# A gated cross-attention block with a mixture of experts on one core: PE sums the expert terms of three tiles, ACT copies the sums out, and the four engines get a new order of work

## What is computed

```python
x = x + tanh(g_xattn[0]) * xattn(layernorm(x), ctx, ctx, Wq, Wk, Wv, Wo)       # 16 heads of 64, causal
x = x + tanh(g_ffn[0]) * ffn(layernorm(x), ...)
# ffn, row by row:
h = rmsnorm(x, gamma1); q = h @ Wq + bq; k, v = split((h @ Wdown + bdown) @ Wup + bup)   # (rows, 16, 8) each
att = softmax(einsum('bthd,btgd->bthg', q, k) / sqrt(8)); out = einsum('bthg,btgd->bthd', att, v)
x = x + (out @ Wo + bo)
h2 = rmsnorm(x, gamma2); gate = softmax(h2 @ Wg + bg)
return x + einsum('btd,edf,bte->btf', h2, We, gate)                            # We is 8 x 128 x 128
```

## Time and profile before

| what | us |
|---|---|
| median of 3 runs | 265.44 |
| lowest and highest | 265.3 and 267.71 |
| the profiled execution's own time | 265.66 |
| its span, first to last instruction | 263.8 |

### The profile page before, as it was taken

The page is one execution under the profiler, slowest core; times in us unless marked ns, Lnnn a source line. Parts: engine busy times, 40 slices in busy tenths (PEclk is TensorE's granted clock), DMA queues, the critical chain, the costliest instruction groups (busy, mean ns, idle before and its releaser), DMA issues.

```text
span 263.8 us, 7717 instructions
## 1 busy us (share of the span) xinstructions
PE 236.0 (89%) x3154; PEld 167.0 (63%) x3154; DVE 195.0 (74%) x335; ACT 168.3 (64%) x498; POOL 159.0 (60%) x169
## 2 busy tenths in 40 slices
PE   5989989898999999998999999989999988851781
PEld 3765778586768585857676776867685665530360
DVE  0236644198989796979798832989897999999925
ACT  2437634756686868785877778667868767651452
POOL 4104041619196877878587376691968778739644
PEclk9999999999999999999999999999999999995698
DMA  6990000000000000000000000000000000000000
GB/s 212 369 307 6 2 4 0 6 0 2 0 5 10 2 14 0 4 10 5 11 2 12 2 10 4 10 5 0 2 12 2 11 4 14 0 0 0 12 10 20
DMA packets 6016, 7.28 MB, mean 28 GB/s; under 512 B 477, under 2 KB 4830, under 8 KB 5982
## 3 DMA queue, kind: packets, MB, share of 16 engines
q1 hardware_dynamic: 5550, 6.16, 7.2%
q10 hardware_dynamic: 432, 0.64, 0.7%
HBM read 5.88 MB, written 0.92 MB: 26 GB/s over the span
## 4 chain that ended last, share of the span: by engine, by line
PE 77%; ACT 9%; DVE 7%; issue 3%; DMA 1%; POOL 0%; SPq 0%; DVEq 0%; ACTq 0%; POOLq 0%
PE ps_a L825 47%; PE ps_c L825 11%; PE ps_b L825 9%; PE ps_e L825 5%; PE ps_b L877 3%; ACT exb L462 2%; DVE ps_e L616 2%; DMA cT<-in_ctx_t 1%; ACT probs L407 1%; ACT probsT L414 1%; ACT v_sb L396 1%; DVE psums L583 1%; PE ps_c L921 1%; DVE exb L684 1%; ACT aT L401 1%
## 5 line engine op out<-in xcount | busy, mean ns | idle before, releaser
L268 POOL TENSOR_TENSOR probs<-probs,prinv 120x672 f32<-120x672 f32 x16 | 24.3, 1517 | 48.3 <-DVE prinv L587 48.2
L277 POOL TENSOR_TENSOR prod<-fqkv 128x1280 f32<-128x1280 f32 (+1 forms) x14 | 38.5, 2752 | 1.9 <-DVE fqkv L601 0.7
L825 PE MATMUL ps_a<-aT,wo_sb 128*128 128x112 f32 x256 | 32.9, 281 | 2.1 <-ACT aT L401 1.3
L825 PEld LDWEIGHTS ps_a<-aT,wo_sb 128*128 128x128 f32 x256 | 29.9, 191 | 4.2 <-ACT aT L401 2.0
L644 DVE TENSOR_REDUCE ps_e<-prod 128x128 f32<-128x2048 f32 x14 | 31.9, 2281 | 0.4 <-POOL prod L288 0.4
L616 DVE TENSOR_REDUCE ps_e<-prod 128x256 f32<-128x2048 f32 x14 | 32.0, 2284 | 0.0
L825 PE MATMUL ps_a<-wv_sb,cT 128*64 128x512 f32 x128 | 31.4, 606 | 0.0
L825 PE MATMUL ps_a<-cT,wk_sb 128*128 128x224 f32 x128 | 28.9, 379 | 1.3 <-DMA cT<-in_ctx_t 1.3
L401 ACT COPY aT<-ps_a 128x448 f32<-128x448 f32 x32 | 15.5, 536 | 20.4 <-PE ps_a L825 20.4
L825 PEld LDWEIGHTS ps_a<-cT,wk_sb 128*128 128x128 f32 x128 | 24.6, 203 | 5.6 <-DMA cT<-in_ctx_t 2.9
L825 PE MATMUL ps_a<-xT,wqc 128*128 128x224 f32 x128 | 27.0, 359 | 0.6 <-ACT qT L390 0.6
(11 more groups left out here) (136 smaller groups left out, 468.9 us busy)
## 6 DMA issues: line engine op xcount, KB each, us to landing
xp_sb<-in_xp SPq DMA_DIRECT2D x1, 896.0 KB, 7.8
out<-out_sb SPq DMA_DIRECT2D x14, 64.0 KB, 1.5
xT<-in_x_t SPq DMA_DIRECT2D x1, 784.0 KB, 9.1
cT<-in_ctx_t SPq DMA_DIRECT2D x1, 784.0 KB, 10.6
wv_sb<-in_wv SPq DMA_DIRECT2D x1, 512.0 KB, 7.7
wo_sb<-in_wo SPq DMA_DIRECT2D x1, 512.0 KB, 12.1
fwe_sb<-in_fwe SPq DMA_DIRECT2D x1, 512.0 KB, 8.8
fw_sb<-in_fw SPq DMA_DIRECT2D x1, 266.0 KB, 12.4
```

The lines of the kernel that those rows point to most:

```text
L268: nc.gpsimd.tensor_tensor(pr[0:TG, NC:C, :, 0:S], pr[0:TG, NC:C, :, 0:S], prinv[p % 2][0:TG, NC:C, :].unsqueeze(3).to_broadcast([TG, C - N ...
L277: nc.gpsimd.tensor_tensor(prod1[:, 0:hp, :, :], t[:, D:2 * D].rearrange("p (g d) -> p g d", g=FH).unsqueeze(1).to_broadcast([128, hp, FH, ...
L825: return nc.tensor.matmul(o, lhsT, rhs, start=start, stop=stop, skip_group_check=True)
```

## The change

1. PE takes over `outputs` for tiles 10, 11 and 12 (`PE_OUT`): `output_sums(f)` runs ten matmuls, the identity against each of the ten terms of `exb`, which add up in one PSUM region (`ps_a` for tile 10, `ps_e` for the others), and ACT copies the sum to `out_sb` (`late_out`). POOL's twelve instructions for the three tiles are gone. Tile 11's sums stand on PE between `turn_x2` and `gate_logits` of tile 13, and tile 12's at the very end.
2. The ten identity matmuls of `stay_warm` are gone.
3. The last tile's gate exponentials are written to PSUM, so `last_gating` reads them there.
4. The slots are put in another order. Steps 2 to 13: PE runs `first` behind `turn_probs` and both expert halves behind `attend`, the upper one first, `shift` ahead of `bias_o`; ACT makes `x1_copy` behind `turned_probs`, and `kv_copy` between the two halves of `experts`; DVE runs `gate_logits` behind `weighted` and `head_sums` ahead of `gate_sum` and `scaled_qkv`; POOL runs `weighted` ahead of `first_scale`. Steps 14 and 15 and the end likewise, as the rows below and the diff show.

The diff, cut to its core (the products' new helper functions hold the same operands as before):

```diff
+PE_OUT = (10, 11, 12)
-STAY_WARM = 10
...
+        def gate_exp(f):
+            return ps_c[:, 1, 256 + E:256 + 2 * E] if f == NT - 1 else gexp[f % 2][:, :]
+
+        def out_sum(f):
+            return ps_a[:, 1, 0:D] if f == PE_OUT[0] else ps_e[:, 0, 0:D]
...
+                elif f in PE_OUT:
+                    sp.wait_ge(s["late_out"], f - PE_OUT[0] + 1)
...
             products(prior)
             first_scale(last)
+            products(last)
             weighted(prior)
-            products(last)
             second_scale(third)
-            outputs(third - 1)
             gating(third)
             weighted(last)
             second_scale(prior)
-            outputs(third)
+            last_residual(last)
             gating(prior)
             second_scale(last)
-            last_residual(last)
-            outputs(prior)
...
+            def late_out(f):
+                act.wait_ge(s["out_summed"], f - PE_OUT[0] + 1)
+                act.wait_ge(stored[f % 2], 16 * (f // 2))
+                nc.scalar.copy(out_sb[f % 2][:, :], out_sum(f)).then_inc(s["late_out"], 1)
...
+            x1_copy(last)
             o_copy(third)
-            x1_copy(last)
+            x2_copy(third)
+            kv_copy(last)
             head_exps(prior)
-            x2_copy(third)
+            late_out(PE_OUT[0])
             squares(third)
-            kv_copy(last)
+            head_exps(last)
             gate_exps(third)
             o_copy(prior)
-            head_exps(last)
+            experts(third, 1)
+            x2_copy(prior)
             squares(prior)
-            experts(third, 1)
+            o_copy(last)
             experts(third, 0)
-            x2_copy(prior)
+            squares(last)
             gate_exps(prior)
-            o_copy(last)
+            x2_copy(last)
             experts(prior, 1)
-            x2_copy(last)
-            squares(last)
             experts(prior, 0)
             gate_exps(last)
+            late_out(third)
             experts(last, 0)
+            late_out(prior)
...
-                nc.vector.tensor_scalar(gate[f % 2][:, :], gexp[f % 2][:, :], ginv[f % 2][:, :], r2[f % 2][:, :],
+                nc.vector.tensor_scalar(gate[f % 2][:, :], gate_exp(f), ginv[f % 2][:, :], r2[f % 2][:, :],
...
+            def output_sums(f):
+                pe.wait_ge(s["lo_ready"], f + 1)
+                pe.wait_ge(s["hi_ready"], f + 1)
...
+                for e in range(E + 2):
+                    ins = mm(out_sum(f), ident[:, :], exb[f % XB][:, e, :], start=(e == 0), stop=(e == E + 1))
+                ins.then_inc(s["out_summed"], 1)
...
             new_y(NP - 1)
+            first(last)
+            bias_o(third)
             turn_o(third)
-            bias_o(third)
             new_o(third)
-            first(last)
             turn_x2(third)
+            output_sums(PE_OUT[0])
             gate_logits(third)
+            bias_o(prior)
+            expert_half(third, 0)
             turn_o(prior)
+            new_o(prior)
             expert_half(third, 1)
-            bias_o(prior)
-            new_o(prior)
-            expert_half(third, 0)
             turn_x2(prior)
+            gate_logits(prior)
             expert_half(prior, 0)
-            gate_logits(prior)
-            stay_warm(prior)
+            turn_o(last)
             bias_o(last)
-            turn_o(last)
+            new_o(last)
             expert_half(prior, 1)
-            new_o(last)
             turn_x2(last)
+            output_sums(third)
             gate_logits(last)
             expert_half(last, 1)
             expert_half(last, 0)
+            output_sums(prior)
```

More of the change, by code:

```diff
@@ L512, in _ @@
                 if t < NP:
-                    attended(t, 0)
                     attended(t, 1)
+                if fc is not None:
+                    experts(fc, 0)
                 if fa is not None:
@@ L517, in _ @@
                 if fc is not None:
-                    experts(fc, 0)
                     experts(fc, 1)
@@ L789, in _ @@
             last, prior, third = NT - 1, NT - 2, NT - 3
+            new_x1(NP - 1)
             products(prior)
-            new_x1(NP - 1)
             logits(prior)
             new_x2(third)
+            scaled_qkv(last)
             shifted_logits(prior)
-            scaled_qkv(last)
+            products(last)
             weighted(prior)
-            products(last)
-            head_sums(prior)
+            logits(last)
             head_scales(prior)
             gate_logits(third)
+            shifted_logits(last)
+            head_sums(prior)
+            gate_sum(third)
             normed_heads(prior)
-            logits(last)
-            gate_sum(third)
-            shifted_logits(last)
-            new_x2(prior)
             weighted(last)
             head_scales(last)
+            new_x2(prior)
             head_sums(last)
+            normed_heads(last)
             gate_logits(prior)
-            normed_heads(last)
+            new_x2(last)
             gate_sum(prior)
-            new_x2(last)
             gate_logits(last)
@@ L1019, in _ @@
                     turn_o(fc)
-                    bias_o(fc)
                 if t < NP:
@@ L1023, in _ @@
                 if fc is not None:
+                    bias_o(fc)
                     new_o(fc)
```

109 lines of the change are left out of this document (56 added, 53 removed).

## The result

The changed kernel takes 269.19 us (median of 4, 268.2 to 269.66), the kernel before beside it 266.48 (4, 265.3 to 267.71): a ratio of 1.011 with a 95% interval of 1.0068 to 1.0151, slower by 1.1%. (The prediction started from 265.44, the median of three executions; beside the changed kernel it took 1.0 us more.) The profiled execution took 268.92 us with a span of 266.8, against 265.66 and 263.8 before.

A forecast was written before the change was run, and what follows sets the result against it. PE's list was taken to bound the body, DVE the next stretch, a chain through all engines the end. Body -0.9 and end +0.2 gave -0.7 from 265.66, so 265.0, or 264.8 us against the median; range 262.6 to 267.4.

The forecast's parts named there:

- Full steps: Eight body steps with both a first and a third stage: PE's new order costs +0.05 us each, +0.4 us together.
- Step 9: Body step without `first`: `attend` waits uncovered, 3.96 us becomes 4.77, so +0.8 us.
- Steps 2, 3 and 11: Body steps without expert halves: `first` fills the 0.69 us in which PE idled, -2.1 us for the three.
- What hides the rest: Body: waits for POOL, DVE and ACT stay covered, by 0.4 us at `turn_probs` and 0.2 to 0.5 us elsewhere.
- Rival (c): Body margin used up, likely `turn_probs` waiting for POOL or `bias_o` for ACT; eight steps pay, 268.5 us; chance 0.08.
- Rival (f): Body: more gain than reckoned, PE's short stops vanish with the new addresses; below 262.8 us; chance 0.12.
- DVE's stretch: Steps 14 and 15 up to tile 13's heads: DVE's list loses small gate instructions and short waits, -0.6 us, heads at 250.8.
- The last chain: Tile 13's heads to last sum: clock returns at 251 to 254, x2 at 254.0; +0.2 us for the end.
- Rival (b): End: PE's clock comes back later than 254 us, end +1.4 us, launch 265.9 us; chance 0.14.
- a few tenths: Very end: tile 12's sum, copy and store end close to tile 13's last sum and may add this at half clock.
- body: Steps 2 to 13, set by PE's own list: the step terms together come to -0.9 us.

The follow-up runs named there:

- first_early_short: Changed kernel with `first` on PE and `x1_copy` on ACT put back to their old places in steps 2, 3 and 11 alone: 270.15 us, ratio 1.0178.
- before_again: The kernel before, unchanged, run once more as a kernel of its own for a second profile: 267.13 us, ratio 1.004.
- old_to_4_filled: Changed kernel with the old order in steps 2, 3, 4, 11 and 12, and 29 identity matmuls in PE's holes at the end: 263.23 us, ratio 0.9889.
- before_no_dummies_psum: Kernel before with the last tile's gate exponentials in PSUM and without the ten identity matmuls: 264.93 us, ratio 0.9959.
- before_filled: Kernel before with 20 identity matmuls in PE's hole ahead of `turn_o` of tile 12: 267.28 us, ratio 1.0037.
- before_gate_psum: Kernel before with only the last tile's gate exponentials moved to PSUM: 266.47 us, ratio 0.9994.
- short_steps_old_filled: Changed kernel with the old order in steps 2, 3 and 11, and 29 identity matmuls in PE's holes at the end: 264.27 us, ratio 0.9889.

## Why the prediction was wrong

Forecast were 264.8 us and no measurable change, with 262.6 to 267.4 as the range; it is 269.19, 4.4 us above the number (2.7 above the kernel before, run beside it), 1.8 above the range, and slower by just over the 1%. By its own steps:

**Full steps, right.** +0.05 us each was forecast, and each takes 14.15 or 14.16 as before. `attend` is 1.71 us behind `turn_probs` (1.73 forecast).

**Step 9, right:** +0.8 forecast, +0.75 measured.

**Steps 2, 3 and 11, half right.** -0.69 each was forecast. Steps 2 and 11 gave 0.46 and 0.66, step 3 lost 0.82: `first` stands behind `turn_probs`, and its own `fqkv` and probabilities come late because step 2 is short as well (first_early_short took it back to 12.21).

**"What hides the rest", wrong, and the first of the two steps that failed.** The margins (0.4 us for `turn_probs`, 0.2 to 0.5 for `products`) were read from step 7 and were right there: 0.57 and 0.28 measured. But they were taken for all steps. They contain the 2 us of expert halves that a step without a third stage doesn't have, so behind the short steps the margin of `products` was about -1.5 (it ends 5.0 us into step 4, where `logits` could start at 3.5). I had counted these three steps as gains and never asked what their shortness leaves to the next one. That cost 0.82 + 1.12 + 1.25 = 3.2 us. Rival (c) had the mechanism, `turn_probs` waiting for POOL, but put it in all eight steps or none; it came in three. It is also only a part in steps 4 and 12: the other wait, of `shift` for DVE's row maxima, and the moves that lead to it, `shift` ahead of `bias_o` on PE and `weighted` ahead of `first_scale` on POOL, the prediction did not name at all. Putting the last one back took 1.1 us out of step 4 once `first` and `scaled_qkv` were early again. How the 1.1 us that step 4 of the changed kernel lost divide among the moves is open.

**Not in the sum, and a gain.** PE's short stops of 0.6 us in step 6 and 0.9 in step 8 vanished: 14.74 and 15.05 became 14.15. Rival (f) had named this, by new addresses of the code, which no run tested; the 1.5 us hid half of the loss. In before_again, the same kernel, the two stops come to 1.2.

**DVE's stretch, right.** -0.6 was forecast, and the heads of tile 13 end 46.80 us behind the start of step 14 instead of 47.59, -0.8.

**The last chain, wrong, the second step that failed.** Its two ends were sound, or on the dear side. The heads of tile 13 were forecast at 250.8 and x2 at 255.2 at half clock, 4.4 us behind them, and it came 4.38 behind; at full clock 252.9, 2.1 behind, and old_to_4_filled has 1.62. x2 to gate was 5.0 to 5.2 in the forecast, 5.41 at a clock that came back in between and 4.66 at full clock. What failed is the choice between them. I let the clock return at 251 to 254, because before it had returned 5 us after PE began again; it returned at 257.6, 10 us after PE's work at 247.76. One observed return is no rule for another pattern of work. Rival (b), clock later than 254, had the right mechanism and 1.4 us; the measured loss is 1.5 up to the last output of tile 13, and 0.5 more behind it, with tile 12's output and two stores at the very end, which the prediction put at "a few tenths" and left out of its sum. The Trainium skill, "TensorE: Matmul & The Clock Gate", Part 1, holds that throttled is the default and only sustained activity releases it; I read it as speaking against removing dummy matmuls. By that rule, what the runs show: adding 29 of them gave back 3.8 us.

I had weighed that rule against the position of the old dummies (they began after the clock was back), and that observation was right too: before_no_dummies_psum is no slower without them. What counts is not whether those ten matmuls are there, but whether the chain behind the last DVE result runs at a low clock, and the new end had moved matmuls into it.

The sum, term by term (forecast, measured, us): body -0.9, +1.34; DVE's stretch -0.6, -0.79; the last chain and stores +0.8, +2.82; start of the kernel 0, -0.37. Together -0.7 and +3.0.

## What to carry to other kernels

Read a margin in the step that has the least of what hides it, not in the typical one: in a software pipeline, the step behind a short one starts with all the other engines' debts. When an order moves on several engines, write each engine's queue down to the last operation that the next step waits for; here one swap that mattered was between two small operations and one of 1.8 us on the engine that looked idle, and another was a wait that an operation had covered until it was moved behind it. Before a rewrite takes matmuls out of an end, see which matmuls will lie uncovered behind the last result of the other engines, and price them at both levels of the clock; in the two ends that were filled here, filling PE's waits paid only where such matmuls lay.

## What the hardware showed that I had not expected

PE can be busy without a pause and still be at the lower level of its clock for some time. In before_filled it was busy for 3.00 of 3.00 us from 238 to 241 at 0.50 (1.2 GHz). In the changed kernel it was busy for 4.76 of 6 us from 250 to 256, all at 0.50.

The small DVE instruction with a PSUM operand is not held up by POOL's addition (0.28 beside 1.54 us in before_gate_psum, 0.28 beside 1.53 in before_no_dummies_psum), while the one with all operands in SBUF ended with it (1.13).

The short stops of PE in steps 6 and 8 (14.74 and 15.05 us) are in every kernel with the old order of the full steps, between 14.44 and 15.06 us, and in none with the new one but for a step 8 of 14.27 (short_steps_old_filled). The profile gives no releaser for them. What causes them is open; together they are worth 0.9 to 1.5 us, more than most terms of my sum.
